# The routed product's unit loops written out on four engines, and the first stage's choice and row scaling moved, in a two-layer attention and feed-forward kernel

## What is computed

```python
x = x + _L0_xattn_ref(_layernorm(x), ctx, W, b)          # q = W x + b; softmax(q ctx^T) ctx
x = x + _L0_ffn_ref(_layernorm(x), gate_w, sh_*, rt_*)   # shared SwiGLU + routed SwiGLU
x = x + _L1_xattn_ref(_layernorm(x), ctx, ctx, Wq, bq, Wk, bk, Wv, bv)
x = x + _L1_ffn_ref(_layernorm(x), W_in, b_in, W_out)    # 8 decision trees of 255 nodes
```

```python
logits = x @ gate_w
top_val, top_id = max(logits), argmax(logits)
score = sigmoid(top_val)
xs = x * score
g, u = xs @ rt_gate[e], xs @ rt_up[e]
y = (silu(g) * u) @ rt_down[e]      # e = top_id, the others are masked out
out = shared + y
```

## Time and profile before

| what | value |
|---|---|
| median of 3 runs (lowest to highest) | 844.21 us (843.31 to 844.83) |
| the profiled execution's own time | 848.09 us |
| its span, first to last instruction | 846.3 us |
| mean granted TensorE clock | 0.986 |
| PE busy | 787.2 us (93%) |
| PEld busy | 637.4 us (75%) |
| DVE busy | 656.0 us (78%) |
| ACT busy | 541.0 us (64%) |
| POOL busy | 266.2 us (31%) |
| share of PE in the chain that ended last | 65% |

### The profile page before, as it was taken

The page is one execution under the profiler, slowest core; times in us unless marked ns, Lnnn a source line. Parts: engine busy times, 40 slices in busy tenths (PEclk is TensorE's granted clock), DMA queues, the critical chain, the costliest instruction groups (busy, mean ns, idle before and its releaser), DMA issues.

```text
span 846.3 us, 15269 instructions
## 1 busy us (share of the span) xinstructions
PE 787.2 (93%) x4452; PEld 637.4 (75%) x4493; DVE 656.0 (78%) x1742; ACT 541.0 (64%) x948; POOL 266.2 (31%) x308
## 2 busy tenths in 40 slices
PE   5899998987877999899999999999999999999997
PEld 4788776776776899877777777777777777777775
DVE  5888889787842456768888888888888888888774
ACT  3577667565321333457786777778677777867765
POOL 2333222887285325003312321331232133121000
PEclk9999999999998999999999999999999999999999
DMA  6346774743333334110000000000000000000000
GB/s 170 90 136 191 193 222 130 202 130 85 88 107 117 109 97 116 51 38 14 26 6 21 25 25 0 25 25 4 21 25 25 0 25 25 4 21 14 14 1 25
DMA packets 91428, 55.88 MB, mean 66 GB/s; under 512 B 13439, under 2 KB 88055, under 8 KB 91255
## 3 DMA queue, kind: packets, MB, share of 16 engines
q1 hardware_dynamic: 75440, 41.29, 17.4%
q0 software_dynamic: 4096, 8.40, 3.5%
q10 hardware_dynamic: 11847, 5.64, 2.4%
HBM read 32.23 MB, written 23.07 MB: 65 GB/s over the span
## 4 chain that ended last, share of the span: by engine, by line
PE 65%; DVE 7%; issue 3%; ACT 3%; another core or an unknown queue 2%; POOL 1%; DVEq 1%; ACTq 0%; POOLq 0%
PE PS L1068 7%; PE PS L823 7%; PE PS L1090 7%; PE PS L1092 7%; PE PS L1091 6%; PE PS L1069 6%; PE PS L1070 6%; PE PS L808 5%; PE PS L1079 4%; PE PS L1009 3%; PE PS L1077 2%; PE PS L992 2%; PE PS L977 2%; DVE xn L1149 1%
## 5 line engine op out<-in xcount | busy, mean ns | idle before, releaser
L765 ACT ACTIVATE sil<-PS,b_in_c 128x512 f32<-128x512 f32 x256 | 162.0, 684 | 93.6 <-PE PS L1077 61.1
L1525 DVE TENSOR_TENSOR sil_l<-sil,sil_h 128x512 fp32r<-128x512 f32 x256 | 164.8, 686 | 48.6 <-ACT sil_h L773 48.6
L526 POOL TENSOR_TENSOR ve<-mv,eps 128x4 f32<-128x4 f32 x64 | 18.9, 295 | 442.2 <-DVE mv L1143 441.6
L773 ACT ACTIVATE sil_h<-sil 128x512 fp32r<-128x512 f32 x224 | 128.9, 631 | 0.0
L1090 PE MATMUL PS<-sil_h,wout_l 128*128 128x512 f32 x256 | 118.8, 464 | 1.7 <-DVE sil_l L1525 1.6
L1068 PE MATMUL PS<-x4T_h,win_l 128*128 128x512 f32 x256 | 102.4, 400 | 1.6 <-ACT yo L725 0.7
L1092 PE MATMUL PS<-sil_h,wout_h 128*128 128x512 f32 x256 | 100.9, 394 | 0.0
L1091 PE MATMUL PS<-sil_l,wout_h 128*128 128x512 f32 x256 | 100.3, 392 | 0.0
L1509 DVE TENSOR_SCALAR dec<-PS,b_in_c 128x512 bf16<-128x512 f32 x128 | 95.4, 746 | 6.2 <-PE PS L1070 4.4
L1069 PE MATMUL PS<-x4T_l,win_h 128*128 128x512 f32 x256 | 99.9, 390 | 0.0
L1070 PE MATMUL PS<-x4T_h,win_h 128*128 128x512 f32 x256 | 99.9, 390 | 0.0
(11 more groups left out here) (169 smaller groups left out, 1550.8 us busy)
## 6 DMA issues: line engine op xcount, KB each, us to landing
x_sorted<-zeros SPq DMA_DIRECT2D x4, 1280.0 KB, 6.8
xs_in<-x_sorted SPq DMA_DIRECT2D x20, 256.0 KB
y_sorted<-yo ACTq DMA_DIRECT2D x20, 256.0 KB
X<-in_x SPq DMA_DIRECT2D x16, 256.0 KB
rows<-xn SPq DMA_DIRECT2D x16, 256.0 KB
out<-res SPq DMA_DIRECT2D x16, 256.0 KB
ctxT<-in_ctx_t SPq DMA_DIRECT2D x16, 240.0 KB
ctx_rows<-in_ctx_kv SPq DMA_DIRECT2D x16, 240.0 KB
```

What stands on the lines that cost most here:

```text
L765: act.activation(tile(sil[p % 2], c, W), bank(2 * (p % 2) + c), ACT.Silu, bias=b_in_c[:, 2 * p + c:2 * p + c + 1]).then_inc(t_silu, 1)
L773: act.activation(tile(sil_h[p % 2], c, W), tile(sil[p % 2], c, W), ACT.Copy).then_inc(t_hi, 1)
L1525: dve.tensor_tensor(tile(sil_l[p % 2], c, W), tile(sil[p % 2], c, W), tile(sil_h[p % 2], c, W).bitcast(F32), ALU.subtract).then_inc(t_lo, 1)
```

## The change

- The `Fori` loops over the units on TensorE, ScalarE, VectorE and the sync queue are written out; waits are against constants. TensorE hands a unit's experts on from unit to unit, where the loop loaded those of two units at the start of each pass.
- The first stage's logits are taken in four quads of 4 groups: (0,4), (4,4), (8,4), (12,4), where the second was 3 groups and the third 1.
- Choice 0 is split: its first three instructions (`choose_tops`) at the end of body 7, the other three (`choose_experts`) at the end of body 8. Choice 1, now 16 tiles, is made at the end of body 10; body 9 has none.
- ScalarE's `score(0)` moves within body 11 from its end to right behind the two copies of the counts, ahead of `xnT`. POOL's `scale(0)` moves from body 12 to the end of body 11.
- The scales of groups 1 to 7 move from POOL to ScalarE, four ACTIVATEs a group, between `K0T` (or `probT`) and `xnT` in bodies 12 (two groups), 13 (one), 14 (two), 15 (one) and 16 (one). POOL's scatters wait for `k_act` in place of its own `k_scaled`. The second half's scales stay on POOL.
- `probT` of body 12 is copied by VectorE, not ScalarE.

```diff
-QUADS = ((0, 4), (4, 3), (7, 1), (8, 4), (12, 4))
+QUADS = ((0, 4), (4, 4), (8, 4), (12, 4))
...
-        ROUTES = {HG - 1: "choose0", HG + 1: "choose1", HG + 2: "choose2", HG + 3: "count", NG + 1: "pack", NG + 2: "all"}
+        ROUTES = {HG - 1: "choose0", HG: "choose0", HG + 2: "choose1", HG + 3: "count", NG + 1: "pack", NG + 2: "all"}
...
+        SCALED_IN = {HG + 4: (1, 2), HG + 5: (3,), HG + 6: (4, 5), HG + 7: (6,), HG + 8: (7,)}
...
         def turned_by_act(g):
-            return HG + 1 <= g <= HG + 3
+            return HG + 1 <= g <= HG + 2
...
             all_scattered(sp, NG)
-            with sp.Fori(HR // 2 - 1, NR // 2 - 1) as i:
-                for u in range(2):
-                    r_next(2 * i + u, u, 1)
+            for r in range(HR - 2, NR - 2):
+                r_next(r, r % 2, 1)
...
             def scatter(t, h, end):
-                v = (t // G) % XB
-                if t % G == 2 and t // G + 1 < end:
-                    scale(t // G + 1)
-                pool.wait_ge(k_scaled, t // G + 1)
+                k = t // G
+                v = k % XB
+                if h and t % G == 2 and k + 1 < end:
+                    scale(k + 1)
+                if 0 < k < HG:
+                    pool.wait_ge(k_act, k)
+                else:
+                    pool.wait_ge(k_scaled, k - HG + 2 if h else 1)
...
-                    pool.wait_ge(scored, 1)
-                    scale(0)
                     pool.wait_ge(placed, 1)
...
+                if route == "count":
+                    pool.wait_ge(scored, 1)
+                    scale(0)
...
+            def scale(k):
+                v = k % XB
+                act.wait_ge(k_in[v], 16 * (k // XB + 1))
+                for j in range(G):
+                    i = act.activation(tile(xs[v], j), tile(xs[v], j), ACT.Identity,
+                                       scale=SCORE[:, k * G + j:k * G + j + 1])
+                i.then_inc(k_act, 1)
...
                         act.activation(ahead, COUNTS_IN[0][0], ACT.Copy).then_inc(r_read, 1)
+                        score(0)
+                for k in rows:
+                    scale(k)
+                if f is not None:
                     act.wait_ge(a_xnT_ps, f + 1)
                     act.activation(xnT, bank(2), ACT.Identity, bias=1.0).then_inc(a_xnT, 1)
...
-                if route == "count":
-                    score(0)
...
-            r_body(0, 0, None)
-            with act.Fori(0, HR // 2 - 1) as i:
-                r_body(2 * i + 1, 1, i)
-                r_body(2 * i + 2, 0, i)
-            for r in range(HR - 1, NR):
+            for r in range(NR):
                 r_body(r, r % 2, (r - 1) // 2)
...
-            r_body(0, 0, None, first_experts)
-            with pe.Fori(0, HR // 2 - 1) as i:
-                now, coming = r_body(2 * i + 1, 1, experts_of(pe, 2 * i))
-                r_body(2 * i + 2, 0, now, coming)
-            pe.wait_ge(routed, 2)
-            now, coming = experts_of(pe, HR - 2), None
-            for r in range(HR - 1, NR - 1):
+            now, coming = r_body(0, 0, None, first_experts)
+            for r in range(1, NR - 1):
+                if r == HR - 1:
+                    pe.wait_ge(routed, 2)
                 now, coming = r_body(r, r % 2, now, coming)
...
-                if route in ("choose0", "choose1", "choose2"):
-                    a_choose(int(route[-1]))
+                if route == "choose0":
+                    choose_tops(0) if f == HG - 1 else choose_experts(0)
+                if route == "choose1":
+                    a_choose(1)
...
-            with dve.Fori(1, HR) as r:
-                coming = r_first(r)
-                r_second(r, coming)
-            for r in range(HR, NR - 1):
+            for r in range(1, NR - 1):
```

More of the change, by code:

```diff
@@ L343, in phase_a @@
                 body(stage(f), stage(f - 1), stage(f - 2), stage(f - 3), f % 2,
-                     range(CALLS[k], CALLS[k + 1]) if 0 <= k < len(CALLS) - 1 else (), ROUTES.get(f))
+                     range(CALLS[k], CALLS[k + 1]) if 0 <= k < len(CALLS) - 1 else (), ROUTES.get(f),
+                     SCALED_IN.get(f, ()))
         def turned_by_act(g):
-            return HG + 1 <= g <= HG + 3
+            return HG + 1 <= g <= HG + 2
         def quad_of(m):
@@ L546, in scatter, with a_body @@
                                         tile(xs[v], t % G), None).then_inc(scattered[v], 16)
-            def a_body(f, g, l, m, u, calls=(), route=None):
+            def a_body(f, g, l, m, u, calls=(), route=None, rows=()):
                 if f is not None:
@@ L1240, in a_body @@
                     take_logits(m, 5)
-                    a_choose(4)
+                    a_choose(3)
                     r_weights(1, 1, experts_of(dve, 0))
                 if route == "pack":
-                    a_choose(3)
+                    a_choose(2)
                 else:
@@ L1321, in _, with quad_cols, choose_tops @@
             keeps = [c_rout[:, C_KEEP - C_RANK + E * B0[h]:C_KEEP - C_RANK + E * (B0[h] + HBS[h])] for h in range(HALVES)]
-            def a_choose(q):
-                h = half_of(q)
-                start, n = (QUADS[q][0] - G0[h]) * G, QUADS[q][1] * G
-                lg, ld, oh, oh_b = (a[:, start * E:(start + n) * E] for a in (LG[:, :], lead, onehot, onehot_b))
-                tp, bs = top[:, start:start + n], best[:, start:start + n]
+            def quad_cols(q):
+                start, n = (QUADS[q][0] - G0[half_of(q)]) * G, QUADS[q][1] * G
+                return (n, *(a[:, start * E:(start + n) * E] for a in (LG[:, :], lead, onehot, onehot_b)),
+                        top[:, start:start + n], best[:, start:start + n])
+            def choose_tops(q):
+                n, lg, ld, oh, oh_b, tp, bs = quad_cols(q)
                 if q == 0:
                     dve.wait_ge(w_late, 16 * len(LATE_W))
-                if q == 3:
+                if q == 2:
                     dve.wait_ge(scored, 1)
@@ L1337, in a_choose, with choose_experts @@
                 step(dve.tensor_tensor(te(ld), te(ld), rank.unsqueeze(1).to_broadcast([P, n, E]), ALU.mult))
+            def choose_experts(q):
+                n, lg, ld, oh, oh_b, tp, bs = quad_cols(q)
                 step(dve.tensor_reduce(bs, te(ld), AX.X, ALU.max))
@@ L1342, in a_choose @@
                     i.then_inc(r_oh, 1)
+            def a_choose(q):
+                choose_tops(q)
+                choose_experts(q)
             def a_counts():
```

4 lines of the change are left out of this document (2 added, 2 removed).

## The result

The change makes the kernel faster, by less than half of the forecast. On the chip of the first measurement the kernel before takes 843.72 us (median of 20 runs) and the kernel after 837.77 (20 runs, 834.45 to 843.52): ratio 0.9937, 95% interval 0.9918 to 0.9956, 5.9 us where 16.8 were forecast.

What follows compares the result with a forecast made beforehand. TensorE, busy for 93% of the span, was taken as the bound. Routed product −13.8 and first stage −3.0 make −16.8 us: from the median of 844.21 to 827.4, range 822.5 to 842.

Steps and rivals of the forecast that it cites:

- Units 2 to 8: Routed product's looped units: written out, 57.3 us falls towards 41.0, with 2.5 given back; −13.8 us, bounds 0 and −16.3.
- the give-back: Routed product: loss remaining beside scatters, three stretches at the 0.84 us of one unit beside gathers; 2.5 us.
- cover: Routed product: last scatter at 277.1 us, unit 10's rows at 283.6; TensorE waits some 0.9, contained in the 2.5.
- First stage, −3.0: Stage before the routed product: terms (a) to (e) sum to −3.1, taken as −3.0 us, bounds −5 and +3.
- (a): First stage, choice 0 split over two bodies: the same 1.68 us in two parts, −0.1 for slack.
- (b): First stage: body from 111.51 us loses logits and a choice, −2.0; the next chooses 16 tiles, +0.6.
- (c): Counting body: score 0 ahead of xnT makes VectorE wait 0.6 us where it waited 0; +0.6.
- (d): First stage: POOL no longer scales groups 1 to 7, scale 0 a body earlier; −2.8 us, bounds 0 and −4.
- (e): First stage: ScalarE takes these scales, 1.45 us a group; +0.3 for probT's copy, +0.3 for late rows.
- Rival 1: Routed product: scatters, not loops, hold TensorE; units 2 to 8 stay, only the first stage pays; 841.2 us, chance 0.18.
- its half (833): Routed product: scatters hold half of TensorE's loss there, so −8.2 and −3.0 us; 833, chance 0.08.
- Rival 2: Routed product: code fetches beside scatters stall written-out units 1 to 8; four fetches, 8.2 us, giving 849.4; chance 0.06.

Runs made afterwards that it cites:

- i1: Kernel before without the second half's scaling, scatters and the row loads that feed them, loops kept: 832.0 us, ratio 0.9953.
- i2: Kernel before with only the four unit loops written out, as e1 but on another chip: 832.26 us, ratio 0.9956.
- e1: Kernel before with all four unit loops (TensorE, VectorE, ScalarE, sync queue) written out, first stage as it was: 832.37 us, ratio 0.996.
- e3: Kernel before with TensorE's unit loop alone written out: 832.98 us, ratio 0.9963.
- e4: Kernel after, unchanged, run again on another chip: ratio 0.9897 to the kernel before.
- i3: Kernel after with POOL's scale of group 9 moved to ScalarE: 825.91 us, ratio 0.9883 to the kernel before.
- g1: Kernel after with POOL scaling groups 1 to 7 as before: 831.17 us, ratio 0.9951 to the kernel before.
- g4: Kernel after, unchanged, run again for a third profile: 828.01 us, ratio 0.9907 to the kernel before.
- h1: Same kernel as i3 (group 9 scaled by ScalarE in the kernel after), on a slower chip: 841.55 us, ratio 0.9917 to the kernel before.
- e2: Kernel after with the four unit loops put back, so only the first stage's changes: 829.28 us, ratio 0.9923 to the kernel before.
- g3: Kernel before, unchanged, run again for a third profile: 836.0 us, ratio 1.0007.
- f4: Kernel before with only the four quads, choice 0 whole in body 7 and choice 1 in body 10: 833.4 us, ratio 0.9968.
- g2: Kernel after with ScalarE's first score back at the end of body 11: 827.35 us, ratio 0.9903 to the kernel before.
- h3: Kernel before, unchanged, run again on a slower chip: 850.3 us, ratio 1.0011.
- f1: Kernel before, unchanged, run again for a second profile: 836.2 us, ratio 0.9998.

## Why the prediction was wrong

**The step that failed** is the routed product's: "Units 2 to 8: 57.3 − 41.0 = 16.3 is the upper bound of the gain; the lower is 0 … so I give back 3 × 0.84 = 2.5: −13.8 us". It charged to the loops what one trace had lost. That trace is one execution, 4.4 us above its chip's median of 20, and it holds two costs that one trace can't separate. The loop's own is 0.22 us a unit (i1, i2), some 1.6 for seven units, and 3.4 for all that e1 changes. The rest is late completions. They come on chips A and E and on none of B, C, D and F; they come in written-out code as well (48.5 us on E, 44.8 on A, where 41.0 is undisturbed), and there the give-back is 7.5 and 3.8, not 2.5. For the seven units the whole change gives 1.7 of the 13.8 on D (42.66 to 40.99), 8.1 on E and 12.6 in the pair of traces on A.

The row from which the give-back was taken was misread. The unit of 6.69 does not run wholly beside POOL's gathers: the last one is issued at 321.77, before the unit begins, and the next at 329.56, behind its end. Its 0.84 is itself a late completion, found on A and E only, and so no measure of what gathers or scatters cost. That the pair of traces nevertheless shows 13.0 of the 16.8 us is luck of two executions. The lower end of the range, 822.5, is 822.9 by the prediction's own terms (844.2 − 16.3 − 5).

**Unit time, last scatter, cover.** Undisturbed written-out units take 5.86 (e1, e3, e4) and the last scatter came within 0.8 us of its forecast. Unit 8, with 7.50 us, did not wait for unit 10's rows, as forecast, but for one last late completion (ScalarE goes on at 278.37 with a Silu whose products end at 277.27). The forecast wait, 0.9, is there where nothing is late and unit 1 was short: TensorE waits 0.61 for these rows in i3 and 0.50 in g1, and not at all in e4 and g4, where unit 1 takes 9.8. Unit 1 does not stay at 8.61: in the kernel after it takes 8.2 us on A and 9.8 on B, D and E, and without POOL's scale of group 9 it takes 6.8 on F (i3) and 8.2 on E (h1). The prediction took that line for fixed.

**First stage, −3.0.** On chip B it is 6.4 (e2). From the first of the eight windows (at 87 to 89 us) to the start of unit 1 the traces of before and after differ by 4.9 us on D (g3, g4), 2.5 on A and 2.0 on E, so here, too, part of the gain is missing on A and E. (a) is 0 where −0.1 was forecast: 12.40 and 12.09 (g4) for 13.08 and 11.40 (g3). (b) is −1.2 by f4, where −1.4 was forecast. (c), +0.6, is 0 at the same clock (g2 and e2). In the trace of after the sigmoid's ACTIVATE stands right behind the load, at 139.13, where the load ends at 139.12. The drain of 1380 ns that the Trainium skill (ScalarE: Activation LUTs, section What ACT_TABLE_LOAD costs) puts beside each load does not show here, neither behind this load nor ahead of it, where the copy before it ends at 137.82. (d) and (e) are −2.2 together, and g1 gives 3.2; but g1 is compared with the kernel after, and its longest collision (4.31 us for xn) is in no trace of before. What the prediction had wrong in (d) is the price of a collision: it counted the idle time alone, 0.96, without the half-clock products behind it (8.67 against 6.08 us). The ScalarE scales themselves cost what was said: 1.27 to 1.30 us a group where 1.45 was forecast, and rows that came late once, for 0.5.

**Rivals.** Rival 1 (scatters hold TensorE and not the loops, 841.2) is right that most of the 16.3 us was not the loops' own. That scatters do it is not shown, and it is too pessimistic in size; 837.8 lies between its half (833) and itself. A pass of TensorE's loop costs 0.44 us in units 2 to 8 (two units of 0.22), and e3 measures 3.1 for all that goes with the loop. The Trainium skill (Advanced Engine Details and Errata, section Control Flow Timing) has about 108 ns for a compare-and-branch, by which the prediction estimated 0.4 us for four passes. No row here times a branch, but a pass costs four times that: the registers with wait values and experts belong to it, though no run separates them. Rival 2 (code supply) finds no support where nothing is late: written out on chips B and F, TensorE is busy for all of 41 us. On E h3 stands still within the loop as well; that fetches add to it there is not excluded.

**What stays open:** why completions are late on two chips of six; whether without scatters they would be on time there; what the loops alone are worth there; and the half of e1's 3.4 us that lies outside units 2 to 8, of which some 0.4 is unit 1 (9.79 against 10.14 in g3 and 10.23 in f1).

## What to carry to other kernels

A stretch that is slow in one trace is priced by a second execution, if possible on another chip, before it is charged to the code: here the same kernel took 42.7 and 56.6 us for the same seven units. Look who is released in the same moment: if two engines go on together, late, it is the sender that is late, and the receivers' loops are not the place to look. A row from which a small loss is taken as a price should be compared with the same unit in another trace: here its loss was the very thing that had to be explained. And a collision of VectorE with POOL is priced with what TensorE's clock does behind the idle time, not by the idle time alone: moving seven small scales from POOL to ScalarE was worth as much as four loops (3.2 and 3.4 us).

## What the runs showed of the hardware

- Six chips ran the same program at 836 (four) and at 844 and 849 us (two). In the kernel before the difference lies where TensorE works beside POOL's scatters: 56.6 against 42.7 in seven units (h3 and g3), while the spans differ by 11.7 and the eight first-stage windows by 0.2. The times of the kernel before spread over 8.7 and 8.9 us on the two slower chips, over at most 4.2 on the others.
- What TensorE had finished by the profile reached ScalarE and the sync queue 4 us later, in the same moment (262.83 in h3), and TensorE stood still for 0.3 to 0.5 us between products that waited for nothing. In five traces on the two slower chips copies of xsT were up to 5.3 us late; in 15 traces on the other four, none of 300 was late by more than 0.05.
- VectorE on 8 and on 40 numbers a partition took 1.07 and 1.65 us instead of 0.17 and 0.20 beside one POOL multiply of 1.05, and four xn took 4.31 instead of 1.1. The Trainium skill (SBUF — State Buffer, section SBUF: two separate sides) describes a port pair that GpSimd and some VectorE instructions (in a two-port mode, or with two inputs in SBUF) lock for a whole instruction, the other blocking. The ends fit it (142.39 beside the scale's 142.36, 228.32 beside 228.25); one start does not, as VectorE's multiply begins at 226.67, 0.52 us ahead of POOL's row. In the stretch of 4.31 POOL's scatters and its addition stand in the row as well.
- Idle time of 1.38 us on TensorE was followed by products at nearly twice their duration (1.91 for 1.06, granted clock 0.52 in f1), idle time of 0.43 was not (1.00 in e4). The length of one idle time doesn't decide it: behind 2.56 us in e2 eight products took 1.16, as at a clock of 1.00, and the eight like them behind another 0.77 took 1.92, at 0.50. The same window up to body 12's xnT took 13.35 us at a granted clock of 1.00 (e2) and 14.81 at 0.88 (e4).
